# Quantised q: converted on its way into SBUF by GpSimd's DMAs, or loaded and converted by VectorE

## What is computed

```
im = relu(x) as [C, N*H*W];  mn = mean over positions;  p = u.T @ (im - mn)
p  = clip(p, -clamp, clamp), quantised to 256 levels per channel between its own min and max
p  = u @ p;  x1 = p - mean(p) + mn                       # end of layer 0, back to [N, C, H, W]
h  = relu(bn(w_conv1 @ x1));  d = relu(bn(w_dr @ h + b_dr))          # 256, then 128 channels
cov = covariance of d over the positions of a sample (128 x 128)
r  = per channel products of bn(cov) with w_row; att = sigmoid(w_fc @ r + b_fc)
out = x1 * att                                           # one factor per sample and channel
```

## Time and profile before

| | us |
|---|---|
| timed runs | 2007.89, 2001.63, 2007.59; median 2007.59 |
| profiled execution | 2002.28 |
| its span, first to last instruction | 2000.3 |
| PE, DVE, ACT, POOL busy in the span | 1683.9, 1471.1, 1425.2, 460.3 |

### The profile page before, as it was taken

How to read it: one execution, slowest core, us unless ns; L and a number is a source line. 1 busy time by engine, 2 the same in 40 slices (tenths; PEclk the granted TensorE clock), 3 DMA queues, 4 the chain that set the end, 5 groups by cost and what they waited for, 6 DMA issues and landing times.

```text
span 2000.3 us, 39033 instructions
## 1 busy us (share of the span) xinstructions
PE 1683.9 (84%) x13394; PEld 1317.5 (66%) x13394; DVE 1471.1 (74%) x2633; ACT 1425.2 (71%) x2046; POOL 460.3 (23%) x135
## 2 busy tenths in 40 slices
PE   8999999999942000059999999999999999999998
PEld 8999999999931000036666666666666666666664
DVE  6888888888865443358878787777778787777774
ACT  6777777777755775646777777777777777777776
POOL 7888888888810000000000000000000000000000
PEclk9999999999965555579999999999999999999999
DMA  9999989989968999920423223242423223242414
GB/s 333 374 350 336 372 313 371 369 313 377 371 280 339 391 424 424 423 84 17 161 81 140 100 108 132 80 161 80 161 80 142 99 111 130 80 161 80 161 66 194
DMA packets 95806, 438.60 MB, mean 219 GB/s; under 512 B 8480, under 2 KB 9632, under 8 KB 80672
## 3 DMA queue, kind: packets, MB, share of 16 engines
q1 hardware_dynamic: 95776, 438.21, 57.1%
HBM read 219.82 MB, written 218.37 MB: 219 GB/s over the span
## 4 chain that ended last, share of the span: by engine, by line
PE 50%; DVE 5%; issue 1%; ACT 0%; DMA 0%; DVEq 0%
PE y_ps L836 15%; PE z_ps L786 14%; PE d_ps L816 14%; PE cov_ps L800 4%; DVE hl L961 2%; DVE g L947 1%; DVE gg L953 1%; PE ch_ps L844 1%; PE ch_ps L826 0%; DVE gg L955 0%; PE ch_ps L827 0%; DMA q<-q_scratch 0%; PE cov_ps L803 0%; ACT yo L895 0%; DVEq L989 0%
## 5 line engine op out<-in xcount | busy, mean ns | idle before, releaser
L268 POOL TENSOR_TENSOR xl<-xs,xh 128x1568 fp32r<-128x1568 f32 x128 | 459.4, 3590 | 97.2 <-ACT xh L228 97.2
L895 ACT ACTIVATE yo<-y_ps,att_cy 128x512 f32<-128x512 f32 (+2 forms) x448 | 313.9, 723 | 138.8 <-PE y_ps L836 128.0
L867 ACT ACTIVATE h<-z_ps,sb_h 128x512 f32<-128x512 f32 (+2 forms) x448 | 277.1, 634 | 73.5 <-PE z_ps L786 63.6
L786 PE MATMUL z_ps<-qr,wh 128*128 128x512 f16 (+2 forms) x896 | 314.4, 354 | 1.4 <-DVE qr L913 1.4
L836 PE MATMUL y_ps<-qr,udh 128*128 128x512 f16 (+2 forms) x896 | 313.5, 353 | 2.3 <-ACT yo L895 1.8
L786 PE MATMUL z_ps<-qr,wl 128*128 128x512 f16 (+2 forms) x896 | 314.2, 354 | 0.0
L836 PE MATMUL y_ps<-qr,udl 128*128 128x512 f16 (+2 forms) x896 | 313.0, 352 | 0.0
L228 ACT ACTIVATE xh<-xs 128x1568 fp32r<-128x1568 f32 x128 | 194.2, 1517 | 140.1 <-PE pp L285 140.0
L816 PE MATMUL d_ps<-vh,hh 128*128 128x128 f16 (+1 forms) x1600 | 282.3, 220 | 10.4 <-DVE hl L961 10.4
L947 DVE SCALAR_TENSOR_TENSOR g<-d_ps,late 128x512 f32<-128x512 f32 (+1 forms) x224 | 141.9, 634 | 198.6 <-PE d_ps L816 194.8
L816 PE MATMUL d_ps<-vh,hl 128*128 128x128 f16 (+1 forms) x1600 | 281.0, 219 | 0.0
(11 more groups left out here) (158 smaller groups left out, 2716.1 us busy)
## 6 DMA issues: line engine op xcount, KB each, us to landing
xs<-in_x_dram SPq DMA_DIRECT2D x128, 784.0 KB, 6.8
out_dram<-yo SPq DMA_DIRECT2D x31, 3136.0 KB, 9.2
pt<-p_scratch SPq DMA_DIRECT2D x56, 1568.0 KB, 11.0
p_scratch<-po_low SPq DMA_DIRECT2D x56, 784.0 KB, 7.8
p_scratch<-late SPq DMA_DIRECT2D x56, 784.0 KB, 7.8
q<-q_scratch SPq DMA_DIRECT2D x32, 784.0 KB, 5.0
q_scratch<-qt SPq DMA_DIRECT2D x28, 784.0 KB, 11.4
q_scratch<-q_res SPq DMA_DIRECT2D x8, 392.0 KB, 11.9
```

The costliest lines, as they stand in the source:

```text
L268: nc.gpsimd.tensor_tensor(xl[:, k % 2], xs[:, k], xh[:, k % 2].bitcast(F32), ALU.subtract).then_inc(split_done, 1)
L786: last = nc.tensor.matmul(z_ps[:, m, 0:w], part[:, k, m * P:(m + 1) * P], qr[:, a, k, columns(s)], start=k == 0 and part is wh, stop=k == ...
L867: nc.scalar.activation(h32[:, par, m, 0:w], z_ps[:, m, 0:w], ACT.Relu, bias=sb_h[:, m:m + 1]).then_inc(z_read, 1)
L895: nc.scalar.activation(yo[:, slot, m, columns(c)], y_ps[:, m, 0:widths[c]], ACT.Identity, scale=att_cy[:, m, 0:1], bias=att_cy[:, m, 1:2]) ...
```

## The change

q is quantised to a signed byte around the middle level instead of an unsigned one above the lowest. In the third stage GpSimd issues one DMA per chunk that reads int8 from `q_dram` and writes float16 into `qr`; it waits for the same output chunks as the conversion did. `q8`, its loads and the conversions are gone, and TensorE waits for the DMA of its chunk, on one semaphore per slot and chunk (14). The mean of q loses its -128.

```diff
-    q_dram = nc.dram_tensor("q_scratch", [N, P, K, M], U8, kind="Internal").ap()
+    q_dram = nc.dram_tensor("q_scratch", [N, P, K, M], I8, kind="Internal").ap()
...
-            qt = sb("qt", [P, 2, K, M], U8, stack=b)
-            q_res = sb("q_res", [P, K, M], U8, stack=b)
+            qt = sb("qt", [P, 2, K, M], I8, stack=b)
+            q_res = sb("q_res", [P, K, M], I8, stack=b)
...
-                nc.vector.tensor_tensor(lo[:], lo[:], shift, ALU.add)
+                settle(nc.vector.tensor_tensor(lo[:], lo[:], shift, ALU.add))
+                nc.vector.scalar_tensor_tensor(out=middle[:], in0=inv[:], scalar=HALF, in1=lo[:], op0=ALU.mult,
+                                               op1=ALU.add)
...
-                        nc.vector.tensor_scalar(qt[:, t // K, t % K], pt[:, t], lo[:, t % K:t % K + 1],
+                        nc.vector.tensor_scalar(qt[:, t // K, t % K], pt[:, t], middle[:, t % K:t % K + 1],
...
-        q_loaded = [sem(f"q_loaded{a}") for a in range(2)]
+        q_cast = [[sem(f"q_cast{a}_{c}") for c in range(CH)] for a in range(2)]
...
-            q8 = cb("q8", [P, 2, K, M], U8)
...
             def _(sp):
-                def load(n, r2, a):
-                    sp.dma_start(q8[:, a], q_dram[n]).then_inc(q_loaded[a], 16)
-
-                load(0, 0, 0)
-                load(1, 0, 1)
-
...
                 def phase(r2, a):
-                    if exists(r2, a, back=1) and exists(r2, a, ahead=1):
-
-                        sp.wait_ge(q_converted, first_chunk(r2, a))
-                        load(2 * r2 + a + 1, r2 + a, 1 - a)
...
-                            pe.wait_ge(q_converted, g + 1)
+                            pe.wait_ge(q_cast[a][s], 16 * r2 + 16)
...
+            @block.gpsimd
+            def _(pool):
+                def cast(n, a, c):
+                    pool.dma_start(qr[:, a, :, columns(c)], q_dram[n, :, :, columns(c)]).then_inc(q_cast[a][c], 16)
+
+                for c in range(LEAD):
+                    cast(0, 0, c)
+
+                def phase(r2, a):
+                    for s in range(CH):
+                        if has(r2, a, s, -LEAD):
+                            if has(r2, a, s, 2 * CH - LEAD):
+
+                                pool.wait_ge(y_done, K * (first_chunk(r2, a) + s + LEAD - 2 * CH + 1))
+                            ahead = s + LEAD >= CH
+                            cast(2 * r2 + a + 1 if ahead else 2 * r2 + a, 1 - a if ahead else a, (s + LEAD) % CH)
+
+                phases(pool, phase)
...
-                def convert(a, c):
-                    nc.vector.tensor_scalar(qr[:, a, :, columns(c)], q8[:, a, :, columns(c)], HALF, None,
-                                            ALU.subtract).then_inc(q_converted, 1)
...
-                nc.vector.tensor_scalar(mq, mq, 1.0 / (N * M), HALF, ALU.mult, ALU.subtract).then_inc(mean_q, 1)
+                nc.vector.tensor_scalar(mq, mq, 1.0 / (N * M), None, ALU.mult).then_inc(mean_q, 1)
...
-                dve.wait_ge(q_loaded[0], 16)
-                for c in range(LEAD):
-                    convert(0, c)
...
-                        if has(r2, a, s, -LEAD):
-                            c = (s + LEAD) % CH
-                            if c == 0:
-                                dve.wait_ge(q_loaded[1 - a], 16 * (r2 + a + 1))
-                            if has(r2, a, s, 2 * CH - LEAD):
-
-                                dve.wait_ge(y_done, K * (g + LEAD - 2 * CH + 1))
-                            convert(a if s + LEAD < CH else 1 - a, c)
```

More of the change, by code:

```diff
@@ L25 @@
 F16 = mybir.dt.float16
-U8 = mybir.dt.uint8
+I8 = mybir.dt.int8
 AX_X = mybir.AxisListType.X
@@ L358, in layer_kernel @@
             pt = sb("pt", [P, TILES, M], stack=b)
-            qt = sb("qt", [P, 2, K, M], U8, stack=b)
-            q_res = sb("q_res", [P, K, M], U8, stack=b)
+            qt = sb("qt", [P, 2, K, M], I8, stack=b)
+            q_res = sb("q_res", [P, K, M], I8, stack=b)
             qa = sb("qa", [P, K], stack=b)
             lo = sb("lo", [P, K], stack=b)
+            middle = sb("middle", [P, K], stack=b)
             hi = sb("hi", [P, K], stack=b)
@@ L552, in resident_tile @@
                     wait_from(dve, res_stored[h], 16 * i)
-                    nc.vector.tensor_scalar(q_res[:, h:h + 1], p_res[:, bass.ds(i, 1), h], lo[:, h:h + 1],
+                    nc.vector.tensor_scalar(q_res[:, h:h + 1], p_res[:, bass.ds(i, 1), h], middle[:, h:h + 1],
                                             qa[:, h:h + 1], ALU.subtract, ALU.mult).then_inc(res_quantised, 1)
@@ L646, in layer_kernel @@
         assert LEAD + Y_LAG < CH
-        q_loaded = [sem(f"q_loaded{a}") for a in range(2)]
+        q_cast = [[sem(f"q_cast{a}_{c}") for c in range(CH)] for a in range(2)]
         out_stored = [sem(f"out_stored{a}") for a in range(2)]
         mean_q, constant_done, bias_done = sem("mean_q"), sem("constant_done"), sem("bias_done")
-        q_converted, z_done, z_read = sem("q_converted"), sem("z_done"), sem("z_read")
+        z_done, z_read = sem("z_done"), sem("z_read")
         hh_done, h_split, d_done, d_read = sem("hh_done"), sem("h_split"), sem("d_done"), sem("d_read")
```

## The result

The changed kernel takes 2026.84 us (four runs, 2025.07 to 2031.35), the kernel before in runs of the same period 2005.2 (2001.63 to 2007.89): a ratio of 1.0114, with a 95% interval of 1.0092 to 1.0136. I had forecast 2004 and no change that can be told.

The account below looks back on a forecast made before the run. TensorE was taken to bound the last stage. Terms of -0.7 - 0.5 + 0 = -1.2 us, taken from 2004.9 us, the middle of four runs, gave 2003.7, say 2004; range 1997 to 2036.

Parts of the forecast that it names:

- Bound and critical loop: Last stage, steady state: TensorE bounds, conversions lie beside its work, so 4.3 us less VectorE work per sample gains 0.
- Start of the stage: Start of last stage: first `z` waits only for TensorE's constants, no longer for load and conversion; gain 0.70 us.
- Second sample: Second sample of last stage: the conversion right before the read of `d_ps` goes; gain 0.5 us, once.
- GpSimd's cost per cast: Last stage: GpSimd needs 1.2 us per cast, between bounds of 0.40 and 3.59; covered.
- The landing of a cast: Last stage: a cast lands 3.6 us after issue; with 1.2 before it, 4.8 of chunk 0's 9.2 us room; cost 0.
- the sum: Whole kernel: gains at the stage's start and in the second sample, casts at 0: -0.7 - 0.5 + 0 = -1.2 us.
- Rival 1: Last stage, chunk 6: casts take turns with an output store and land late; 0.75 us per sample, +22 us, 2026; chance 0.16.
- Rivals 2, 3 and 4: Last stage: GpSimd and VectorE hinder each other, +36 us, 0.11; casts over 4.94 us, +237, 0.07; VectorE's relief, -7, 0.12.

Follow-up runs that it names:

- before_thin_convert: The kernel before, with VectorE converting only 16 of a chunk's columns from the third sample on: ratio 0.9998.
- chunk_stores: The changed kernel, with the output stored per chunk, 7 stores per sample instead of one: 2000.94 us, ratio 0.9987 to the kernel before; run again, 0.9992.
- one_row_casts: The changed kernel, with each cast moving the same bytes in 128 rows instead of 256, output permuted: 2002.06 us, ratio 0.9984 to the kernel before.
- two_stores: The changed kernel, with a sample's output stored as chunks 0 to 2 and chunks 3 to 6: 2006.6 us, ratio 0.9998 to the kernel before.
- plain_copies: The changed kernel, with GpSimd's DMAs copying bytes without conversion from the third sample on, output different: 2004.37 us, ratio 0.9998 to the kernel before.

## Why the prediction was wrong

**Bound and critical loop: right.** TensorE bounds the stage, and its one old wait stays, 0.2 us per sample. In `before_thin_convert` 2.9 of the 4.3 us of VectorE's work per sample are gone, in `chunk_stores` all of them, and neither gains anything that can be measured.

**Start of the stage: right.** TensorE's first `z` follows the constant products, at 868.85 against 869.35. The gain is 0.5 us instead of 0.70, since the stage itself starts some 0.2 us later. In the chain of the changed kernel:

```profile
866.98 1.87 PE cov_ps L762 x8
868.85 3.45 PE z_ps L778 x8
```

**Second sample: right in kind.** The read of `d_ps` follows `r` at once (0.70 from 916.39), with nothing between, where the conversion of the earlier trace rows stood.

```profile
916.32 0.05 DVE r L985
...
916.39 0.70 DVE g L952
```

**GpSimd's cost per cast: right side, smaller.** 0.71 us instead of 1.2. The queue takes another 0.6 us between the end of the output chunk and the issue at chunk 6 (1202.48 to 1203.10), which I hadn't counted.

**The landing of a cast: the step that failed.** I wrote "1.2 + 3.6 = 4.8 us of the 9.2: covered, cost 0", with the price of a cast alone on the DMA engines. For five chunks in seven that price is on the safe side (2.6 to 2.9 us measured). Chunk 0's cast met the store's second half and took 5.3 us, still inside the 9.2. For chunk 6 the price is that of a cast issued with the store: 10.0 us where the sum had 3.6. The room I gave, 10.4 us, was from one `z` start to the next; counted from the end of the output chunk's last matmul, which lies some 0.2 us behind the next start, it is 10.2, and 0.62 + 9.97 + 0.12 us to start `z` are 10.7. The missing half microsecond, and the 0.2 us by which the idle pipeline starts late, are the 0.74 us per sample.

**Rival 1 was the case.** I gave it 0.16, with 0.75 us per sample, +22 us and 2026; measured were 0.74, 22 and 2026.84. Its mechanism, one for one turns with the store, is shown by the packet counts and borne out by `one_row_casts` and `two_stores`. It had the size for partly wrong reasons, and that the figures agree to 0.01 us per sample is luck: it took 16 turns from the cast's start, 9.9 us, where 4 packets of the store per engine went ahead and 12 turns followed, 10.0; it took 1.2 us to the issue where it was 0.6; and it took the start of the next `z` as the end of the output. What I set against it was a bad comparison: the loads of 784 KB that landed in 4.3 to 6.6 us were issued 6.7 us after the store by the same queue and only met its end. The row nearest to a small DMA in company was the 11.9 us store of `q_res`, which I named for the rival but kept out of the sum. And the trace before does not show what a converting DMA's packets look like, so that 16 rows per engine might have been two turns, as in `plain_copies`, or 16; the sum had no place for this, and the rival took the right one without a reason. Where two cases 20 us apart depend on such a point, 0.16 was too little.

**Rivals 2, 3 and 4: out.** `hl` lasts 1.22 us as before, though GpSimd issues casts beside it (1203.10 to 1203.81 against `hl` from 1203.21), so it isn't held back. The fp16 cast lasts 0.43 us as before, but in this sample it ends (1202.57) before GpSimd's issue begins (1203.10), so whether casts would wait for it is not shown. No cast is over 4.94 us of GpSimd's time, and none but those beside a store over that on the engines. Relief gives nothing that can be measured.

## What to carry to other kernels

Before moving a small transfer with a due time to another queue, list the big transfers that are in flight when it is issued, and price it in packets. As an estimate from these runs: the packets of the big one that each DMA engine moves before the small one's first (4 for the changed kernel's chunk 6, 5 in `plain_copies`, none in `one_row_casts`), plus one for each packet of the small one, each at the duration of a packet of the big one; it ends at the latest with the big one or a little behind. If that is over the room, cut or delay the big transfer (by chunks, as it gets ready) or give the small one fewer and longer rows. And work taken from an engine is worth what it takes off a wait, not its busy time: 139 us off VectorE were worth 1 or 2, within the noise.

## What the runs showed of the hardware that I had not expected

A converting DMA from GpSimd sends every row as a packet of its own, a plain one groups the 16 rows of an engine into two packets: 272 against 48 packets per DMA of 256 rows, semaphore increments included. Alone the difference is hardly seen (2.6 to 2.9 against 2.4 to 2.6 us to landing); beside a store of 12.5 KB packets it is 10.0 against 6.3 us (the plain copy writes half the bytes). The order of issue on two queues isn't the order of the packets: the cast of chunk 6, issued 0.2 us before the store, had its first packet 3.0 us after its issue, behind 4 of the store's per engine, while the cast of `one_row_casts`, also issued 0.2 us before the store, had it 1.2 us after and went first. And GpSimd's issue depends on the rows: 0.53 us for 128, 0.71 for 256 (the group's means in `one_row_casts` and in the changed kernel).

```profile
L901 POOL DMA_DIRECT2D qr<-q_scratch x224 | 118.4, 532 | 1279.4 <-PE y_ps L832 959.3 <-POOLq L357 306.3 <-issue 13.9
```
